# Attention with the query norm as a row, squares summed by feature, short products in one group, and the second rotation sum on GpSimd

## What is computed

```python
q = _causal_dwconv(_silu(x @ Wq), conv_q_w); k = ...; v = ...; z = x @ Wz; a = x @ Wa; b = x @ Wb
q, k, v = (u.reshape(Bc, Sc, 16, 128) for u in (q, k, v))          # 16 heads
q = q * cos + rot_half(q) * sin;  k = k * cos + rot_half(k) * sin
q = q / jnp.maximum(jnp.linalg.norm(q, axis=-1, keepdims=True), 1e-12);  k = the same
for s in range(4):                                                  # the token and the three before it
    attn = jnp.einsum('bshd,bshd->bsh', q, lag(k, s)) * scale
    out = out + (attn * jax.nn.sigmoid(lag(a, s) * b))[..., None] * lag(v, s)
out = out.reshape(Bc, Sc, 2048)
rms = jax.lax.rsqrt(jnp.mean(out * out, axis=-1, keepdims=True) + EPS_NORM)
out = out * rms * norm_w * _silu(z)
return out @ Wout
```

## Time and profile before

| | |
|---|---|
| Median of 3 runs | 2850.29 us (2849.97 to 2850.31) |
| The profiled execution | span 2847.8 us from its first to its last instruction; what lies around it has no row, the median is 2.5 us above the span |
| PE busy | 2826.6 us, 99% |
| DVE, ACT, POOL busy | 2252.7, 1528.7, 1443.2 us (79%, 54%, 51%) |
| Granted TensorE clock | 0.999 of full speed (2.4 GHz) in the mean |
| DMA | 160.44 MB, engines 18.5% busy with the kernel's queue |

### The profile page before, as it was taken

The page is one execution under the profiler, slowest core; times in us unless marked ns, Lnnn a source line. Parts: engine busy times, 40 slices in busy tenths (PEclk is TensorE's granted clock), DMA queues, the critical chain, the costliest instruction groups (busy, mean ns, idle before and its releaser), DMA issues. The chain is left out here.

```text
span 2847.8 us, 40066 instructions
## 1 busy us (share of the span) xinstructions
PE 2826.6 (99%) x13466; PEld 2348.4 (82%) x13466; DVE 2252.7 (79%) x3265; ACT 1528.7 (54%) x3149; POOL 1443.2 (51%) x1016
## 2 busy tenths in 40 slices
PE   9999999999999999999999999999999999999998
PEld 7888888888788888888888888778778887888887
DVE  7899587777888889888988898977667677666665
ACT  6656333333666666666666666765545445444443
POOL 7787233334344444444444444666545556555554
PEclk9999999999999999999999999999999999999999
DMA  3000000000322222222222221321111111211111
GB/s 138 1 23 25 12 19 27 30 27 23 125 65 68 70 64 64 65 73 64 64 64 72 77 71 53 93 75 52 52 45 52 60 45 56 86 45 60 52 52 45
DMA packets 79099, 160.44 MB, mean 56 GB/s; under 512 B 11313, under 2 KB 19889, under 8 KB 77873
## 3 DMA queue, kind: packets, MB, share of 16 engines
q1 hardware_dynamic: 78896, 157.88, 18.5%
HBM read 115.63 MB, written 8.65 MB: 44 GB/s over the span
## 5 line engine op out<-in xcount | busy, mean ns | idle before, releaser
L1546 DVE SCALAR_TENSOR_TENSOR x_tok<-OP,expert_weight,x_tok 128x512 f32<-128x512 f32 x252 | 188.1, 748 | 138.2 <-PE OP L47 138.1
L1425 POOL TENSOR_TENSOR middle_w_lo<-second_raw,middle_w_hi 128x512 fp32r<-128x512 f32 (+1 forms) x96 | 143.4, 1496 | 208.7 <-ACT middle_w_hi L1420 208.7
L1518 POOL TENSOR_TENSOR middle_in_lo<-middle_slot,middle_in_hi 128x512 fp32r<-128x512 f32 x128 | 168.6, 1318 | 131.7 <-ACT middle_in_hi L1514 130.9
L3017 POOL TENSOR_TENSOR lag_rnorm<-lag_norm,minus_half 128x8 f32<-128x8 f32 x64 | 105.1, 1643 | 209.5 <-DVE lag_norm L3408 209.5
L45 PE MATMUL B<-xT_hi,lag_w_hi 128*128 128x512 f32 x516 | 201.4, 390 | 1.8 <-DVE xT_lo L496 1.5
L47 PE MATMUL B<-xT_hi,lag_w_lo 128*128 128x512 f32 x516 | 201.6, 391 | 0.0
L45 PE MATMUL A<-xT_hi,lag_w_hi 128*128 128x512 f32 x512 | 200.6, 392 | 0.4 <-DVE xT_lo L496 0.4
L46 PE MATMUL B<-xT_lo,lag_w_hi 128*128 128x512 f32 x516 | 200.8, 389 | 0.0
L47 PE MATMUL A<-xT_hi,lag_w_lo 128*128 128x512 f32 x512 | 199.9, 390 | 0.0
L46 PE MATMUL A<-xT_lo,lag_w_hi 128*128 128x512 f32 x512 | 199.4, 389 | 0.0
L45 PE MATMUL OP<-middle_down_hi,middle_in_hi 128*128 128x512 f32 x496 | 193.6, 390 | 1.9 <-POOL middle_down_lo L1445 1.7
(11 more groups left out here) (670 smaller groups left out, 9103.8 us busy)
## 6 DMA issues: line engine op xcount, KB each, us to landing
lag_raw<-in_head_weights SPq DMA_DIRECT2D x64, 256.0 KB, 4.5
lag_b_row<-lag_b_scratch SPq DMA_DIRECT2D x64, 256.0 KB, 3.3
lag_rot_q<-lag_r SPq DMA_DIRECT2D x128, 128.0 KB, 2.3
lag_rot_k<-lag_r SPq DMA_DIRECT2D x128, 128.0 KB, 2.4
middle_down_raw<-in_expert_down SPq DMA_DIRECT2D x32, 512.0 KB, 3.4
middle_raw<-in_expert_in SPq DMA_DIRECT2D x32, 384.0 KB, 3.0
second_raw<-in_expert_in SPq DMA_DIRECT2D x32, 384.0 KB, 3.0
double_raw<-in_dense_in SPq DMA_DIRECT2D x12, 512.0 KB, 3.4
```

What stands on the lines that cost most here:

```text
L1425: pool.tensor_tensor(self.w_lo[q % 2][:, out], self.raw[q % 2][:, of], f32(self.w_hi[q % 2][:, out]), ALU.subtract).then_inc(self.s_wlo, 1)
L1518: pool.tensor_tensor(self.inner_lo[q % 3][t], self.slot((1, 3)[t], q), f32(self.inner_hi[q % 3][t]), ALU.subtract).then_inc(self.s_lo, 1)
L1546: dve.scalar_tensor_tensor(row, self.down_bank(v, n), self.expert_weight[:, e:e + 1], row, op0=ALU.mult, op1=ALU.add).then_inc(self.s_acc, 1)
L3017: pool.tensor_tensor(rnorm[f.rbuf], norm2, half[:, 0:2 * TPB], ALU.pow).then_inc(s_rn, 1)
```

## The change

Five edits, all in the attention:

1. The query's norm becomes a row. DVE reduces the squares of a step one slot later (`norm_sums`), POOL takes the power, DVE transposes the 128x32 words of `norms` (`turn_norms`), SP stores the result in five small DMAs to a row in DRAM (`store_query`) and loads it back, broadcast to all partitions, as `query` (`load_query`, 128x524). POOL multiplies it with the band mask (`band_of_query`), and DVE multiplies the gated scores with it (`probabilities`). The output needs no scale any more: `accumulate` is a plain sum in the steps up to 61.
2. The sum of squares for the RMS norm is kept by feature. ACT makes the square instead of a copy when it takes the mixed output out of PSUM (`mixture`), and POOL issues a DMA that adds the 128x512 tile to a sum in DRAM (`add_squares`). Only at the end are the four sums loaded and turned (`turn_sums`). `turn_mixed` and `sum_squares` are left for the last two steps alone.
3. The short products stand in one group: squares, values, `mix` of `l2` and `score` of `l1` follow the two projections, and the `out_projection` of `l2` is one group of four tiles at the slot's end, in banks OP0, OP1, S0, S1. The mix, the gated output and `y` move a slot later.
4. The scores are multiplied with the gate (`gains`) straight from PSUM.
5. The sum `r2 + cross2` is made by POOL, not by DVE.

The core of the diff:

```diff
+                def store_query(st):
+                    sp.wait_ge(s_n2, 3 * st.s + 3)
+                    until(sp, s_query, st.s * 96)
+                    window = query_norm[st.s % 2, :, :]
+                    for g in range(TPB):
+                        sp.dma_start(window[:, g * 32:(g + 1) * 32], turned[g * 32:g * 32 + TPB, :]).then_inc(s_query, 16)
+                    sp.dma_start(window[0:TPB - 1, P:BAND], turned[1:TPB, 0:PAD]).then_inc(s_query, 16)
+
+                def load_query(st):
+                    sp.wait_ge(s_query, st.s * 96 + 80)
+                    until(sp, s_prob, 2 * st.s)
+                    sp.dma_start(lag["query"], query_norm[st.s % 2:st.s % 2 + 1, :, :].rearrange("a t n -> a (t n)")
+                                 .to_broadcast([P, TPB * BAND])).then_inc(s_query, 16)
...
+                    if l1 and l1.s < BY_ROW:
+                        if l1.s == 0:
+                            sp.wait_ge(s_rows, 32)
+                        store_query(l1)
+                        load_query(l1)
+                    sp.wait_ge(s_rotated, 3 * f.s + 3)
                     until(sp, s_s, f.s)
                     sp.dma_start(rot_q[0:64, 0:SEQ], r1[0:64, :]).then_inc(s_move1, 16)
...
                     if l1:
+                        turn_squares(l1)
                         turn_values(l1)
+                        if l2:
+                            mix(l2)
                         score(l1)
...
                         projection(l1, 3, B, s_z)
-                        if f.s < SWITCH:
-                            if l2:
-                                turn_mixed(l2)
-                            mix(l1)
...
+                    if l2:
+                        if f.s == END:
+                            pe.wait_ge(s_mean, 3)
+                        until(pe, s_prob, 2 * l1.s + 1)
+                        out_projection(l2, range(TPB), [OP0, OP1, S0, S1], 4)
...
+                    act.activation(head_out[st.s], O, ACT.Square if st.s < BY_ROW else ACT.Copy).then_inc(s_mix, 1)
...
+                def band_of_query(st):
+                    pool.wait_ge(s_query, st.s * 96 + 96)
+                    pool.tensor_tensor(query[:, :, :], query[:, :, :], band_t.unsqueeze(1).to_broadcast([P, TPB, BAND]),
+                                       ALU.mult).then_inc(s_band, 1)
+
+                def add_squares(st):
+                    pool.wait_ge(s_mix, st.s + 1)
+                    if st.s < WHOLE:
+                        until(pool, s_squares, st.s * 16)
+                        sums = square_sums[st.b * P:(st.b + 1) * P, :]
+                        if st.head:
+                            pool.dma_start(sums, head_out[st.s], accum_op=ALU.add).then_inc(s_squares, 16)
...
                 for f, l1, l2, l3 in slots():
+                    if l2 and l2.s < BY_ROW:
+                        band_of_query(l2)
                     if f.b and f.head + 1 < HEADS:
                         split_head(f.head + 1, 1 - f.wbuf, SPLIT_AT[f.b])
...
                     pool.tensor_tensor(r2, c2, cos, ALU.mult).then_inc(s_cos, 1)
+                    pool.wait_ge(s_cos, f.s * 3 + 2)
+                    pool.wait_ge(s_rotated, 3 * f.s + 1)
+                    pool.tensor_tensor(r2, r2, cross2, ALU.add).then_inc(s_cos, 1)
                     pool.wait_ge(s_sqr, f.s * 2 + 2)
                     pool.tensor_tensor(squares[0], squares[0], squares[1], ALU.add).then_inc(s_pair, 1)
...
+                    elif st.s < BY_ROW:
+                        until(dve, s_acc, st.s * TPB + t - 1)
+                        dve.tensor_tensor(row, out, row, ALU.add).then_inc(s_acc, 1)
...
                 def gains(st):
                     dve.wait_ge(s_gate, st.s + 1)
-                    dve.scalar_tensor_tensor(gate[:, :, :], gate[:, :, :], 1.0,
-                                             band_t.unsqueeze(1).to_broadcast([P, TPB, BAND]),
-                                             op0=ALU.add, op1=ALU.mult).then_inc(s_gain, 1)
+                    dve.wait_ge(s_s, st.s + 1)
+                    dve.scalar_tensor_tensor(gate[:, :, :], gate[:, :, :], 1.0, scores[:, :, 0:BAND],
+                                             op0=ALU.add, op1=ALU.mult).then_inc(s_prob, 1)
...
+                    if st.s < BY_ROW:
+                        dve.wait_ge(s_band, st.s + 1 + (st.s > WHOLE))
+                        dve.tensor_tensor(prob[:, :, :], gate[:, :, :], query[:, :, :], ALU.mult).then_inc(s_prob, 1)
...
+                def turn_norms(st):
+                    dve.wait_ge(s_rn, st.s + 1)
+                    until(dve, s_query, st.s * 96)
+                    dve.transpose(turned, norms[st.rbuf]).then_inc(s_n2, 1)
```

More of the change, by code:

```diff
@@ L1828, in layers @@
         raw1 = overlay("second", [(None, 3 * MAT, F32), ("raw1", 8 * Paired.BLOCK, F32)])["raw1"]
+        of_batch = overlay("sums", [(None, MAT, F32)] + [(f"rows{b}", SEQ, F32) for b in range(BATCH)])
         exact = overlay("exact", [(None, 3 * MAT, F32), ("n40", 2 * SEQ, F32), (None, 4 * MAT - 2 * SEQ, F32), ("n41", 2 * SEQ, F32)])
@@ L1977, in layers @@
         s_o, s_mix, s_ot, s_osq = sem("o"), sem("mix"), sem("ot"), sem("osq")
+        s_query, s_band = sem("query"), sem("band")
+        s_squares, s_rows = sem("squares"), sem("rows")
         s_y, s_yhi, s_ylo = sem("y"), sem("yhi"), sem("ylo")
@@ L3327, in _ @@
                 for f, l1, l2, l3 in slots():
-                    inside = l1 and f.s < SWITCH
-                    if l3 and f.s < END:
-                        accumulate(l3, 2)
-                    if l1:
-                        gains(l1)
-                    if l3 and f.s < END:
-                        accumulate(l3, 3)
+                    if l3:
+                        for t in range(TPB):
+                            accumulate(l3, t)
+                    if l2 and l2.s < BY_ROW:
+                        probabilities(l2)
                     dve.wait_ge(s_tap, f.s * 3 + 1)
@@ L3355, in _ @@
                         norm1.aggregate(dve, 3)
+                    if l2:
+                        gated_output(l2)
+                    tap(1, f, B, c2, 2, s_c2)
+                    tap(1, f, B, c2, 3, s_c2)
+                    if l1:
+                        gains(l1)
+                        if f.s == END:
+                            probabilities(l1)
+                            sum_features(2, OP0)
+                        turn_norms(l1)
+                    if f.s == 1:
+                        factors.take(dve, 3, 3)
@@ L3427, in _ @@
                 accumulate(before_last, 1)
-                rows.low_tile(dve, 0)
-                for t in (1, 2, 3):
+                for t in range(TPB):
                     rows.low_tile(dve, t)
```

360 lines of the change are left out of this document (191 added, 169 removed).

## The result

The changed kernel takes 2858.82 us (median of 5, 2858.31 to 2861.82), the kernel before 2850.31 beside it (2849.97 to 2850.41, 5 runs): ratio 1.0032, 95% interval 1.0019 to 1.0045. It is slower by 8.5 us, where 24 us less were forecast. The profiled execution took 2859.97 us with a span of 2858.2, so its time is 1.8 above its own span, where the prediction added 2.5.

The account below looks back on a forecast made before the run. TensorE (PE), 99% busy at its upper clock, was taken to bound the kernel. Span 2847.8 - 25.5 - 1.2 + 3 = 2824.1, plus 2.5 between span and median, 2826.6, say 2826 us; range 2819 to 2864.

Parts of the forecast that it names:

- 232 x 0.11: TensorE: 232 of the 256 transposes of lag_mixed go, 0.11 us each, saving 25.5 us.
- the slot of 16.30: Steady attention on TensorE: one new slot holds 16.30 us of work, where the kernel before took 16.77.
- the two terms: TensorE's savings: 25.5 us from transposes removed and 1.2 us from one entry to OP fewer in each of 60 slots.
- The blocking: POOL products holding up DVE's probabilities, cross products and r1: charged 3 us over 60 slots, bounds 0 to 22.
- 0.5 us of slack in front of the z projection: Bank B: DVE's taps end at 10.26, TensorE wants it at 10.84; said to just cover probabilities ending 0.45 late.
- the ring: Loop of probabilities, taps, gains, transpose, stores, load, mask product, next probabilities; its length sets the slot if beyond its room.
- The norm's trip: DVE's transpose through five DMA stores and a broadcast load to its landing: 6.7 us, at the bounds 1.9 longer.
- Rival A: Slower: the norm's way round closes a loop through the probabilities and sets the slot; +40 us, 2866 us; chance 0.16.
- rival B: Half the gain lost to POOL blocking DVE, 0.25 us in 45 slots, 0.1 elsewhere; +13, 2839 us; chance 0.15.
- DVE's load of 14.6 a slot: Steady attention: DVE's work falls from 15.0 us a slot by 0.4 to 14.6 of 16.30, leaving room.
- The hand-over: Attention to experts: final sums loaded, added, turned; TensorE's 4.2 us of idle time assumed the same, give or take 4.
- rival D: POOL's DMA issue costs above 4 us, not the 1 taken, making the mask product late every slot; chance 0.04.

Follow-up runs that it names:

- after: The changed kernel itself, with all five edits against the kernel before; 2858.82 us (1.0032).
- e13: Changed kernel with POOL's weight parts waiting for the probabilities, and the last step's work reordered on DVE and POOL at the hand-over; 2831.18 us (0.9934).
- e9: Changed kernel with one more wait: POOL's weight parts (split_head) wait for the step's probabilities, the mask product stays first; 2836.62 us (0.9951).
- e4: Changed kernel with edit 5 undone, the r2 + cross2 sum made by DVE again; 2921.4 us (1.0251).
- e6: Changed kernel with POOL's weight parts ahead of the mask product, and the last step's work reordered on DVE and POOL at the hand-over; 2842.95 us (0.9974).
- e8: Kernel before with edit 5 alone, the r2 + cross2 sum made by POOL; 2851.48 us (1.0004).

## Why the prediction was wrong

**TensorE's work: right.** 232 x 0.11 and the slot of 16.30. The shortest slots of after are 16.28, e13's mean is 16.34, and between its first and last value transposes it has 25.1 us less than before, where the two terms sum to 26.7.

**The blocking, charged at 3 us: the step that failed.** The prediction had the mechanism and the place (the weight parts start right behind the mask product and the probabilities wait), and both ends of its price, 0 to 22, and took 3, since 0.5 us of slack in front of the z projection was to cover it. The slack was looked for at TensorE's next demand. But the probabilities stand on the ring, and a ring has no slack from elsewhere: e9 takes away this one wait and 22.2 us go. That is nearly the whole loss of the steady slots. The prediction's own numbers had it: transpose done at 11.1, mask product done at 19.15, blocked probabilities done 1.95 later at 21.1, and 6.76 more, as from 4.34 to 11.1, make the next transpose done at 27.86. That is 16.76 us round in three slots of four, 0.46 over the slot of 16.30: 45 x 0.46 = 21 us, if the fourth slot takes nothing back. The lateness of 0.45 was read off once and laid against the slack; it should have been followed round. The value's taps were to have room for the cross product's microsecond, and that held: 1.67 us in e9, at no cost.

**The norm's trip: 6.7 forecast, 7.2 measured** (from the end of the transpose; the 7.4 above count from its start). The load was nearly right (3.05 at least, 3.24 in the median, forecast 3.0). The five issues were cheaper (1.33 us from the first start to the fifth, forecast 2.04). The store was mis-sized: from the fifth issue to the load's issue 2.7 us, SP's own steps included, where 1.6 was taken from the best of four; their median of 2.7 was the right row. That leaves half a microsecond too little. It wasn't needed for the loss in the prediction's own terms, where the blocked ring is 16.76 with the short trip. In the measured slot it is near the edge: 16.73 less 0.45 is 16.28, TensorE's own 16.28. What a shorter trip would have given isn't shown; no run shortened it without leaving the norm out. Rival A, the ring, was the mechanism; it was priced at 2866 and given 0.16, and it joined with the blocking of rival B instead of standing beside it. That its price and the measured 2858.82 lie 7 us apart is in part luck: the price stood for 0.9 us in each of 45 slots and nothing behind them, where the measured turns are some 0.45 too long and the hand-over and the end make 10 us.

**DVE's load of 14.6 a slot: too low.** It is 189.87 x 16.76 / 200 = 15.9, of which the two blocked operations make some 1.8. It was near enough to full that e4 could fill it.

**The hand-over, "the same, give or take 4": wrong by twice that.** Up to the last value transposes the changed kernel stands even, and from there to the experts' first matmul 8.1 us are added; the last three slots have 2.8 us more besides (51.7 for 48.9), within the even sum. I had followed the final sums and not the order of the last step's work on DVE and POOL. e6 and e13 take back 3.1 and 5.4 by order alone; the rest of it was not tried.

**The end of the program: a term that the prediction lacks.** From the last matmul to the end of the span it is 8.1 us in before and e8, and 10.0 in after and all fourteen kernels built on it. POOL's closing DRAIN takes 0.66 us in the first two, in which POOL issues no DMA, and 5.58 in the others, in which it issues 60; no run takes the DMAs away and leaves the rest, so their part in it is likely and not shown.

**Right again:** POOL's DMA issue, 0.88 us for the 1 taken, so rival D is out; a transpose of 0.205 for 0.2. The Trainium skill's 3.1 for an issue beside a blocked port (SBUF — State Buffer, the section on a bandwidth pool) was not met in any run here, though no row shows one that ran beside an operation of the kind that it names.

## What to carry to other kernels

When a value leaves an engine and comes back to the same engine's queue one iteration later, add up the ring: the trip, and everything that stands in the queue between its return and its next departure. Its length bounds the iteration, whatever idle time the queue shows. Once it is longer than the busiest engine's work, anything that lengthens a piece of it (a blocked operation, a transfer beside the load, smaller pieces) is paid each time, while the same microsecond off the ring was free here. Order the engine beside it so that it runs against operations off the ring: here one wait, which moved the five weight parts of each head back by one microsecond (2.13 us behind the mask product's start in place of 1.17), was worth 22 us.

## What the runs showed of the hardware

- A DVE operation with two SBUF inputs can be passed by two POOL operations in a row: 2.96 us in e4 for 0.68 alone. The Trainium skill (SBUF — State Buffer, the section on the two sides) gives the port to whichever starts first for the whole instruction; that fits the first POOL operation, and it does not say who is next: here it was POOL's second, though DVE's had been waiting.
- Four moves of 128 KB beside a load of 262 KB delay it by 0.1 to 0.6 us, the more the sooner they follow, and as much when two of them go ahead.
- A trip of 512 words through DRAM, five stores and a broadcast load, takes 7.2 to 7.5 us in the median from the transpose's start to the first use (after 7.4, e9 7.3, e13 7.2), of which no more than 2 are issues.
- A wait at a seam has a price beyond itself: some ten microseconds of after's hand-over ran at 1.2 GHz (0.63, 0.50, 0.84 of the full clock in three stretches of 5 us), where the four transposes of `x_tok` to bank A took 1.12 us (1846.03) and not the 0.60 that they take in before at the full clock (1841.08).
- POOL's closing DRAIN takes 5.58 us in every kernel here in which POOL issued 60 DMAs and 0.66 in the two in which it issued none; the program ends 1.9 us later by it.
